# Two narrow attentions reordered: values before the output projection, the latents' norm in two parts, high halves sent first

## The reference

```python
x = x + _L0_xattn_ref(_layernorm(x), ctx, ctx, Wq, bq, Wk, bk, Wv, bv, Wo, bo)   # 16 heads of 8, 77 keys
x = x + _L0_ffn_ref(_layernorm(x), ...)     # itself: x + mla_attention(rmsnorm(x)); x + moe(rmsnorm(x))
x = x + _L1_xattn_ref(_layernorm(x), ctx, ...)                                   # 8 heads of 64
x = x + _L1_ffn_ref(_layernorm(x), ...)                                          # top 2 of 8 experts

def mla_attention(x, ...):                                       # 16 heads of 8, causal, 128 keys
    q = (x @ Wq.T)...;  latent = layernorm(x @ Wdkv.T, ln_g, ln_b)               # 64 latents
    k = (latent @ Wuk.T)...;  v = (latent @ Wuv.T)...
    q, k = apply_rope(q), apply_rope(k)
    attn = softmax(where(causal, q k^T / sqrt(8), -inf))
    return (attn @ v) @ Wo.T
```

## Time and profile before

| | us |
|---|---|
| median of 3 runs | 1976.58 |
| lowest and highest | 1973.33, 1977.42 |
| span of the profiled execution, first to last instruction | 1970.2 |
| first attention, steady part | about 36 to 388 of the span |
| latent attention, steady part (14 groups) | about 448 to 892 of the span |
| busy in the span: PE, DVE, ACT, POOL | 1504.9, 1354.8, 1174.0, 791.4 |

### The profile page before, as it was taken

The page is one execution under the profiler, slowest core; times in us unless marked ns, Lnnn a source line. Parts: engine busy times, 40 slices in busy tenths (PEclk is TensorE's granted clock), DMA queues, the critical chain, the costliest instruction groups (busy, mean ns, idle before and its releaser), DMA issues. The chain is left out here.

```text
span 1970.2 us, 63623 instructions
## 1 busy us (share of the span) xinstructions
PE 1504.9 (76%) x22193; PEld 1114.2 (57%) x22194; DVE 1354.8 (69%) x3761; ACT 1174.0 (60%) x2992; POOL 791.4 (40%) x836
## 2 busy tenths in 40 slices
PE   3888888838878887878324995888888886699991
PEld 2666666515555555556223782666666665587780
DVE  4778777548777777776553664778788876566665
ACT  2666666615444544445423993987888784477770
POOL 1000000023232322221584562447766666776661
PEclk9999999959999999999556996999999897799995
DMA  2222121000010100010012221001111000233227
GB/s 81 61 59 66 57 60 48 25 17 31 21 34 19 34 20 33 19 33 18 27 42 74 77 67 48 23 23 45 45 33 36 30 31 31 79 92 103 74 75 258
DMA packets 119870, 100.93 MB, mean 51 GB/s; under 512 B 18355, under 2 KB 111030, under 8 KB 119632
## 3 DMA queue, kind: packets, MB, share of 16 engines
q1 hardware_dynamic: 97712, 67.62, 11.8%
q0 software_dynamic: 12928, 25.60, 3.7%
q10 hardware_dynamic: 8992, 4.47, 0.8%
HBM read 43.30 MB, written 32.96 MB: 39 GB/s over the span
## 5 line engine op out<-in xcount | busy, mean ns | idle before, releaser
L2623 POOL DMA_INDIRECT e_back<-e_out_rows,e_G x142 | 150.2, 1057 | 73.1 <-issue 51.1
L1584 ACT ACTIVATE w_weights<-w_pS,w_ng 128x77 f32<-128x77 f32 x512 | 157.9, 339 | 25.5 <-DVE w_ng L1682 25.3
L717 DVE TENSOR_REDUCE m_mx<-m_pM 128x8 f32<-128x1024 f32 x128 | 155.5, 1215 | 22.5 <-PE m_pM L409 22.2
L568 ACT ACTIVATE m_PT<-m_pS 128x1024 f32<-128x1024 f32 x128 | 130.4, 1019 | 59.4 <-PE m_pS L438 58.1
L1192 POOL DMA_INDIRECT e_rows<-re_R,re_index x128 | 128.9, 1007 | 63.5 <-issue 38.8
L568 ACT ACTIVATE a_PT<-a_pS 77x1024 f32<-77x1024 f32 x128 | 130.5, 1019 | 29.3 <-PE a_pS L438 25.3
L2644 DVE TENSOR_TENSOR e_gl<-e_g,e_gh 128x512 f16<-128x512 f32 x142 | 98.3, 692 | 58.6 <-ACT e_g L2599 54.6
L831 POOL TENSOR_SCALAR a_var<-a_aggr 128x4 f32<-128x4 f32 x16 | 3.1, 193 | 307.2 <-DVE a_aggr L643 307.2
L717 DVE TENSOR_REDUCE a_mx<-a_pM 128x8 f32<-128x616 f32 x128 | 101.3, 792 | 34.2 <-PE a_pM L409 34.2
L1804 POOL TENSOR_TENSOR w_weights<-w_weights,w_rec 128x616 f32<-128x616 f32 x64 | 77.9, 1217 | 107.1 <-DVE w_rec L1686 106.8
L1584 ACT ACTIVATION_READ_ACCUMULATOR w_weights<-w_pS,w_ng 128x1 f32 x512 | 113.5, 222 | 0.0
(11 more groups left out here) (401 smaller groups left out, 5688.8 us busy)
## 6 DMA issues: line engine op xcount, KB each, us to landing
e_G<-e_rows SPq DMA_DIRECT2D x106, 132.0 KB, 2.3
e_B<-e_back SPq DMA_DIRECT2D x16, 512.0 KB, 6.9
X<-in_x SPq DMA_DIRECT2D x16, 256.0 KB, 3.0
Qs<-a_qh SPq DMA_DIRECT2D x128, 32.0 KB
Qs<-m_qh SPq DMA_DIRECT2D x128, 32.0 KB
Ks<-m_kh SPq DMA_DIRECT2D x32, 128.0 KB
YW<-e_back SPq DMA_DIRECT2D x16, 256.0 KB, 3.2
w_stage<-in_late SPq DMA_DIRECT2D x16, 256.0 KB
```

The costliest lines, as they stand in the source:

```text
L568: act.activation(PT[:NK, b % 2, 8 * half:8 * half + 8, :], pS[:NK, :, :], ACT.Exp, scale=float(1.0 / np.sqrt(HD))).then_inc(exp_done, 1)
L717: dve.tensor_reduce(out=mx[:, 8 * half:8 * half + 8], in_=pM[:, :, :NK], op=ALU.max, axis=AX.X).then_inc(m_max, 1)
L1584: ac = act.activation(weights[:, b % 2, n, :], pS[:, n // HB, n % HB, :KC], ACT.Exp, bias=ng[:, b % 2, n:n + 1], scale=float(WD) ** -0.5, ...
L2623: pool.indirect_dma_start(out=back, out_offset=bass.IndirectOffsetOnAxis(ap=G[:, r, s, D:D + 1].bitcast(I32), axis=0), in_=out_rows[:, r, ...
```

## The change

Three parts, all in `narrow_attention`.

1. PE: `values` of the step before moves ahead of `project_output`, in both attentions and every step.
2. DVE and POOL: the part of lat is cut in two. The statistics (`latent_stats`) stay in the first slot of b=3; the norming of the rows moves behind `output_lo` and the first `take_max`. In all steps `residual` moves behind the norm statistics (b=0), the norm rows (b=1) and the rms rows (b=2) of the group after next. On POOL the root `squares` moves from behind the low half of K to between the rotated sum of K and its low half.
3. SP: `stack` no longer waits for the low half at its head. It waits for the high half, sends what reads it, then waits for the low half and sends that; the order of K's three DMAs becomes kh, kh, kl.

The four rows of the latents' norm (`m_xn`) have moved down past `m_ol` and the first reduction of the maxima. The diff, without the parts that these rows show:

```diff
         def stack(engine, g, p, what):
-            if what == "q":
-                engine.wait_ge(rope_lo, lin(g, 2, 1)) if latent else engine.wait_ge(evac, use(g, "q") + 1)
-            else:
-                engine.wait_ge(rope_lo, lin(g, 2, 2)) if latent else engine.wait_ge(evac, use(g, "k") + 1)
-            settle(engine, c)
             wait(engine, s_ready, lin(g, 2 * GB, -2 * GB))
             settle(engine, c)
-            for r in range(3):
+            engine.wait_ge(hi_made, hi_count(g, what + "s" if latent else what))
+            settle(engine, c)
+            lows = {"q": 2, "k": 1}
+            for r in (0, 3 - lows[what], lows[what]):
+                if r == lows[what]:
+                    if what == "q":
+                        engine.wait_ge(rope_lo, lin(g, 2, 1)) if latent else engine.wait_ge(evac, use(g, "q") + 1)
+                    else:
+                        engine.wait_ge(rope_lo, lin(g, 2, 2)) if latent else engine.wait_ge(evac, use(g, "k") + 1)
+                    settle(engine, c)
...
                 what, gw, far = slot(b, 0, g, nxt, nxt2)
-                if what:
+                if what == "lat":
+                    latent_stats(gw)
+                elif what:
                     part(what, gw, (p + far) % 2)
                 if two:
                     output_lo(*two)
                 if more:
                     take_max(gn, bn, 0)
-                if two:
-                    residual(*two)
+                if what == "lat":
+                    part(what, gw, (p + far) % 2)
                 if b == 0 and nxt2:
                     norm_stats(shift(g, 2))
                 if b == 1 and nxt2:
                     norm_rows(shift(g, 2))
                 if latent and b == 2 and nxt2:
                     rms_rows(shift(g, 2))
+                if two:
+                    residual(*two)
...
-            def rope(what, g):
+            def rope(what, g, between=None):
                 if what in ("qs", "ks"):
...
                     pool.tensor_tensor(t1[:, k, :], t1[:, k, :], t2[:, k, :], ALU.add).then_inc(rope_sum, 1)
+                    if between:
+                        squares(between)
                     pool.wait_ge(rope_sum, lin(g, 2, 1 + k))
                     pool.wait_ge(hi_made, hi_count(g, what))
...
-                if b == 1 and nxt2:
-                    squares(shift(g, 2))
```

More of the change, by code:

```diff
@@ L500, in step @@
                 scores(g, p, b, 0)
+                if before:
+                    values(gp, pp, bp)
                 if two:
                     project_output(*two)
-                if before:
-                    values(gp, pp, bp)
                 if more:
@@ L694, in part @@
                 elif what == "lat":
[L695 to L701, removed]
                     dve.wait_ge(lat_rstd, lin(g, 1, 1))
@@ L711, in part, with latent_stats @@
                                       ALU.add).then_inc(evac, 1)
+            def latent_stats(g):
+                dve.wait_ge(used, use(g, "lat") + 1)
+                for b in range(GB):
+                    dve.bn_stats(lstats[:, b, :], pP[:, b * LAT:(b + 1) * LAT]).then_inc(lat_st, 1)
+                for b in range(GB):
+                    dve.wait_ge(lat_st, lin(g, GB, b + 1))
+                    settle(dve, c)
+                    dve.bn_aggr(laggr[:, b, :], lstats[:, b, :]).then_inc(lat_agg, 1)
             def take_max(g, b, half):
@@ L772, in begin @@
                         take_max((None, 0), 0, 0)
+                    if what == "lat":
+                        latent_stats((None, k))
                     part(what, (None, k), k)
@@ L891, in step @@
                     if what:
-                        rope(what, gw)
-                if b == 1 and nxt2:
-                    squares(shift(g, 2))
+                        rope(what, gw, shift(g, 2) if what == "ks" and nxt2 else None)
             pool.wait_ge(zeroed, 3)
```

## The result

The changed kernel takes 1909.57 us (median of 4 runs, 1906.33 to 1913.49), the kernel before 1977.0 beside it: a ratio of 0.9661, 95% interval 0.9634 to 0.9688. I had predicted 1928 with a range from 1911 to 1952.

What follows compares the result with a forecast made beforehand. It took the kernel as bound by waits that PE and DVE lay on each other. Gains of 9 + 35 + 5 = 49 us off the 1970.2 us span gave 1921, plus 6.4 to the median: 1928 us, range 1911 to 1952.

Steps and rivals of the forecast that it cites:

- The failed step: First attention, b=0 and b=1: DVE is the bound, so PE's gain is covered and counted at nothing.
- the term of 9 us: First attention, b=2: second maxima come earlier for DVE, 0.65 us in each of 14 groups.
- if the gap moves to the residual: First attention, lower bound of its gain: nothing, if DVE's wait moves to the residual; upper bound 27 us.
- The latent attention: Latent attention: K's earlier landing (1.14 us) and a shorter b=3 (1.39 us) give 2.5 us a group, 35 us.
- For b=2 I had 1.1: Latent attention, b=2: root and residual no longer delay the rms rows, so the transposes of x come 1.1 us earlier.
- from the first maxima to the second reduction: Latent attention, b=3: second reduction at M + 3.75 instead of M + 5.14 after the first maxima, 1.39 us won.
- SP stays the bound: Rival, latent attention: SP's first issue comes no earlier, only b=3 gains; 19 + 9 = 28 us, 1948; chance 0.15.
- The clock: Latent stretch: shorter waits in b=2 and b=3 bring back 5 us of at most 18 lost to the slower clock.
- the clock rival: Rival: the clock stays up and all 18 us come back; 9 + 35 + 18 = 62 us, 1914; chance 0.13.
- `pO`: Rival, steps with a projection: the later projection and residual hold up the next `turn_heads`; 72 us slower, 2049; chance 0.04.
- Behind the two attentions: Stretch after both attentions: no change counted; a move of more than a few us would show the prediction wrong.
- The 6.4 us between span and median: Whole kernel: the median of the runs lies 6.4 us above the profiled span, added to 1921 to give 1928.

Runs made afterwards that it cites:

- DVE's share taken alone: The kernel before with only DVE's residual moved behind the norm statistics, norm rows and rms rows: 1970.76 us, ratio 0.9974.

## Why the prediction was off

**The failed step: b=0 and b=1 of the first attention.** I wrote that "DVE is the bound there", so "what PE gains is covered and I count nothing". This was the term of 9 us, and it came to 19.4. By steps, over the whole attention: b=0 gained 5.1 us, b=1 2.3, b=2 10.9 (forecast 9: 0.69 us a step in the median for 0.65, but in all 16 groups where I had counted 14), b=3 0.4, and the start 0.7, which the run with high halves first alone has as well. So 7.3 us of the 10 that were missing come from the two steps that I counted at nothing, and without them the time would lie in the range. Two things were wrong in the step. First, a DVE without idle time before the statistics is no proof that DVE's time is fixed: the order of its own instructions held 0.34 us in b=0, of which no row shows any as idle. The change moves that order too, and I priced the residual's move only by its 0.28 us in b=2. Second, PE stood only a little behind: with DVE's share taken alone, b=0 gained 0.03 us and PE was last. The values and the residual therefore had to be counted together: 2.0 and 4.5 us alone, 18.6 in one. A sum made edit by edit could not give that, and "nothing" was not even a bound: without the residual's move b=0 and b=1 lose 0.3 and 0.6 us a step. The lower bound of the first attention, "if the gap moves to the residual", is what the values alone show, 2.0 us in all.

**The latent attention.** The steps hold. Groups without a fall became 2.7 us shorter (forecast 2.5): the medians of b=0 to b=2 moved by -0.16, +0.11 and -1.06 us, and b=3 from 8.58 to 6.97, so -1.61. For b=2 I had 1.1, and from the first maxima to the second reduction 1.39 us against 1.37 measured. 14 by 2.7 is 38 us for 35. What the prediction left out is how the parts hang together. High halves first is worth nothing alone and 42 us as the last part; the split is worth some 19 either way. The rival "SP stays the bound" can be held against the run without the high halves, and its 1948 us beside 1951.98 is luck: it had 19 us from the latent attention, which gave 4.4 (488.9 to 484.5), and 9 from the first, which gave 16.1.

**The clock.** Over the 14 groups the gain is 443.8 - 399.4 = 44.4 us, 38 of it the steps, which by subtraction leaves some 6 us for the clock where I took 5. The falls behind the waits of b=2 and b=3 are gone but for one, and three at loop edges stay, much as the prediction had it; the clock rival had all 18 us and is wrong. The Trainium skill, "TensorE: Matmul & The Clock Gate", section "Why this matters for your kernels", says that idle gaps between bursts of matmuls take the clock back to half. The traces agree in kind: 0.50 behind a wait of 4.37 us, 0.98 in the mean without such waits.

**The other rivals.** `pO` did not become the bound: `turn_heads` (L462) waits for the residual for 3.0 us in all in the first attention and never in the latent one. Behind the two attentions the time moved by 2.2 us, which I had as nothing. That stretch, in which little of the two attentions is left, lies between 1037.5 and 1042.7 us in the fourteen profiles (1040.0 before, 1042.3 after), so 2.2 us cannot be told from its spread. The 6.4 us between span and median were luck as well: a run's time lies 2 us above its own span, and the rest was which execution had been profiled.

## What to carry to other kernels

Before an edit is counted at nothing because another engine is the bound, ask whether the same change also moves that engine's order, and by how much the first engine stands behind it; an edit that frees one engine can be worth little alone because it makes the other wait at a new place, and much with the edit that takes this wait away. Where waits follow one another on one chain, price the last one that remains, since removing an earlier one only moves the time there. When a transfer is late because its queue issues a long row, look for an engine that is idle at that moment, and count the issue as busy time of that engine.

## What the runs showed of the hardware that was not expected

- Two issues of DMAs of 128 KB took 1.43 us of ACT's time and kept it from its next instruction for 1.64 us; on POOL two took 1.16 us and landed 2.1 us after their issue in the median; on SP two took 1.22 us.
- An extra semaphore wait in SP's list of issues made a pause of 0.12 to 0.2 us in nearly every group, ahead of Q's low half and of K's, where issues without one followed some 0.05 us apart.
- The same DVE instructions took 2.47 or 2.13 us from reduction to reduction, by their order alone (2.14 in the kernel before with only that order changed), without idle time in the rows.
